# Five edits at the seams of a one-core transformer kernel: the last expert tile's order, the experts' numbers, the picks' weights, layer b's first batch, layer b's last root

## What is computed

```
x = x + attn_a(layernorm(x))        # 16 heads, causal
x = x + ffn(layernorm(x))           # 8 experts, each row goes to 2 of them
x = x + attn_b(layernorm(x))        # one head of 256, its own layernorm inside
x = x + ffn(layernorm(x))           # the same experts again

def ffn(x):
    t = x * rsqrt(mean(x * x) + EPS) * norm_scale
    top_v, top_i = top_k(t @ gate_w + gate_b, 2);  probs = softmax(top_v)
    for each expert e of a row: h = swiglu(t @ mlp1_w[e] + mlp1_b[e])
                                y += probs[e] * (h @ mlp2_w[e] + mlp2_b[e])
    return x + y
```

## Time and profile before

| | us |
|---|---|
| median of 3 runs (lowest, highest) | 1772.99 (1771.53, 1776.3) |
| the profiled execution: its own time | 1772.1 |
| its span | 1770.4 |
| PE busy in the span | 1627.7 (92%) |
| DVE busy | 1277.2 (72%) |
| ACT busy | 1046.8 (59%) |
| POOL busy | 801.5 (45%) |

### The profile page before, as it was taken

How to read it: one execution, slowest core, us unless ns; L and a number is a source line. 1 busy time by engine, 2 the same in 40 slices (tenths; PEclk the granted TensorE clock), 3 DMA queues, 4 the chain that set the end, 5 groups by cost and what they waited for, 6 DMA issues and landing times. The chain is left out here.

```text
span 1770.4 us, 35743 instructions
## 1 busy us (share of the span) xinstructions
PE 1627.7 (92%) x11140; PEld 1195.2 (68%) x11141; DVE 1277.2 (72%) x2668; ACT 1046.8 (59%) x1849; POOL 801.5 (45%) x773
## 2 busy tenths in 40 slices
PE   7889999999999784999999997799965999999997
PEld 3454444444443673999999997445444999999997
DVE  5678788888882686777777775368876777777775
ACT  3336677776777464666666663557653666666664
POOL 5431111112121132666666664225642666666674
PEclk9999999999999895999999999899975999999999
DMA  5755254453431662332322323301112223222232
GB/s 140 187 143 132 86 137 113 112 133 105 121 96 43 163 222 69 65 48 48 48 48 48 48 48 45 96 0 48 48 63 70 42 48 48 48 48 48 47 48 38
DMA packets 102668, 140.85 MB, mean 80 GB/s; under 512 B 18161, under 2 KB 86769, under 8 KB 99505
## 3 DMA queue, kind: packets, MB, share of 16 engines
q1 hardware_dynamic: 65638, 90.88, 19.3%
q0 software_dynamic: 31808, 37.32, 13.3%
q10 hardware_dynamic: 5130, 11.54, 1.9%
HBM read 74.21 MB, written 56.69 MB: 74 GB/s over the span
## 5 line engine op out<-in xcount | busy, mean ns | idle before, releaser
L555 ACT ACTIVATE a_Pt<-a_p_st 128x512 f32<-128x512 f32 (+2 forms) x624 | 301.6, 592 | 131.3 <-PE a_p_st L636 131.2
L582 DVE TENSOR_REDUCE mx<-a_p_sn 128x2 f32<-128x256 f32 (+1 forms) x600 | 332.9, 626 | 61.6 <-PE a_p_sn L619 52.2
L1322 ACT COPY R<-values_then_w 128x1024 f32 x284 | 283.0, 1044 | 41.7 <-issue 21.4
L1273 PE MATMUL e_p_g<-e_tT,R 128*128 128x128 f32 x2272 | 280.2, 277 | 3.4 <-ACT e_tT L1314 3.4
L1273 PE MATMUL e_p_l<-e_tT,R 128*128 128x128 f32 x2272 | 276.9, 275 | 0.0
L1285 PE MATMUL e_p_y<-w,e_hid 128*128 x1136 | 268.9, 380 | 2.3 <-DVE e_hid L1388 2.3
L1273 PEld LDWEIGHTS e_p_g<-e_tT,R 128*128 128x128 f32 x2272 | 268.0, 194 | 4.3 <-ACT e_tT L1314 4.2
L1273 PEld LDWEIGHTS e_p_l<-e_tT,R 128*128 128x128 f32 x2272 | 265.2, 192 | 0.0
L532 POOL TENSOR_SCALAR_AFFINE_SELECT a_Pt<-a_Pt 128x512 f32<-128x512 f32 x128 | 81.6, 637 | 361.9 <-ACT a_Pt L555 361.9
L1285 PEld LDWEIGHTS e_p_y<-w,e_hid 128*128 128x128 f32 x1136 | 205.0, 190 | 25.1 <-issue 3.1
L619 PE MATMUL a_p_sn<-Kst,Qst 96*128 96x128 bf16 (+1 forms) x720 | 219.0, 331 | 1.5 <-PEq L151 1.5
(11 more groups left out here) (211 smaller groups left out, 2375.0 us busy)
## 6 DMA issues: line engine op xcount, KB each, us to landing
qk_parts<-a_part SPq DMA_DIRECT2D x64, 192.0 KB, 3.1
a_Vst<-values_then_w SPq DMA_DIRECT2D x16, 512.0 KB, 18.4
o_rows<-a_OT ACTq DMA_DIRECT2D x32, 256.0 KB, 2.9
values_then_w<-in_mlp SPq DMA_DIRECT2D x16, 512.0 KB, 4.5
t_rows<-R SPq DMA_DIRECT2D x16, 512.0 KB, 3.0
Kst<-qk_parts SPq DMA_DIRECT2D x14, 384.0 KB
Qst<-qk_parts SPq DMA_DIRECT2D x14, 384.0 KB
X<-in_x SPq DMA_DIRECT2D x8, 512.0 KB, 5.4
```

The costliest lines, as they stand in the source:

```text
L555: act.activation(weights(kb, slice(h, h + n), a, b), p_st[:, i % RING, 0:n * (b - a)].rearrange("p (n w) -> p n w", n=n), ACT.Exp, scale=D ...
L582: dve.tensor_reduce(mx[:, hs[0]:hs[-1] + 1, place], p_sn[:, (s + k) % RING, 0:w * len(hs)].rearrange("p (h w) -> p h w", w=w), AX.X, ALU.m ...
L1273: mm = pe.matmul(bank[:, s, c * P:(c + 1) * P], copied[:, s, k, at:at + P], tT[:, s, k * P:(k + 1) * P], start=(k == 0), stop=(k == KD - 1))
L1322: act.copy(copied[:, s, :, cols], g["w1"][:, bass.ds(e, 1), :, cols].rearrange("p a k n -> p (a k) n")).then_inc(copied_done, 1)
```

## The change

- **The last expert tile's order.** In step 70 PE does `down(69)` between the two halves of `up`, and DVE makes `yb(69)` before it adds the bias to p_l. It was after both on either engine.
- **The experts' numbers.** The three instructions that make `expert` stand ahead of DVE's wait for `inv_done`, not at the list's end.
- **The picks' weights.** All weights are gathered by `load` in `experts`; those of tiles 0 and 1 were gathered in `rank`. They count on a semaphore `wt_in` of their own. PE's `rows` waits for the rows alone, and ACT's `result` has one more wait, for `wt_in`. SP waits for `w_out` in POOL's place.
- **Layer b's first batch in halves.** Norm 0's first unit of eight tiles becomes two of four, in statistics, moments, root, coefficients and normals; the later units' numbers go up by one. ACT begins the block with a square root of one element, which nobody reads.
- **Layer b's last root at once.** `deviations(1, B - 1)` stands ahead of `turned_rows(last // 2 + 1)`.

```diff
@@ rank, DVE
+            link(dve.tensor_tensor(tiles[:, :, :], g["ramp"][:, 0:MT].unsqueeze(2).to_broadcast([P, MT, E]),
+                                   cnt[:, 2, :].unsqueeze(1).to_broadcast([P, MT, E]), ALU.is_ge))
+            link(dve.tensor_reduce(fslot[:, :], tiles[:, :, :], AX.X, ALU.add))
+            link(dve.tensor_scalar(g["expert"][:, :], fslot[:, :], float(E - 1), None, ALU.min))
             dve.wait_ge(inv_done, Q // QQ)
...
             link(dve.tensor_tensor(g["result"][:, :], row[:, 1, :], g["spare"][:, :], ALU.add))
-            link(dve.tensor_tensor(tiles[:, :, :], g["ramp"][:, 0:MT].unsqueeze(2).to_broadcast([P, MT, E]),
-                                   cnt[:, 2, :].unsqueeze(1).to_broadcast([P, MT, E]), ALU.is_ge))
-            link(dve.tensor_reduce(fslot[:, :], tiles[:, :, :], AX.X, ALU.add))
-            link(dve.tensor_scalar(g["expert"][:, :], fslot[:, :], float(E - 1), None, ALU.min))
@@ rank, POOL
             pool.wait_ge(token_done, 1)
-            gather_rows(pool, g, t_dram, 0)
-            pool.wait_ge(pick_done, 1)
-            pool.wait_ge(w_out, 16)
-            gather_weight(pool, g, w_dram, 0)
-            gather_rows(pool, g, t_dram, 1)
-            gather_weight(pool, g, w_dram, 1)
+            for j in range(2):
+                gather_rows(pool, g, t_dram, j)
@@ gather_weight
-                            ).then_inc(g["xs_in"][j % 2], 16)
+                            ).then_inc(g["wt_in"][j % 2], 16)
@@ experts, POOL load
                 if j >= 2:
                     pool.wait_ge(tp_done, j - 1)
                     gather_rows(pool, g, t_dram, j)
-                    gather_weight(pool, g, w_dram, j)
+                gather_weight(pool, g, w_dram, j)
@@ experts, PE rows
-                pe.wait_ge(xs_in[s], 16 * (j - s) + 32)
+                pe.wait_ge(xs_in[s], 8 * (j - s) + 16)
@@ experts, PE step
+                if last:
+                    down(j - 1, 1 - s, e, False)
                 up(j, s, 1, p_l, copied_l, l_done, l_read, first)
-                if not begins:
+                if not begins and not last:
                     down(j - 1, 1 - s, e, isinstance(j, int) and j < 3)
@@ experts, ACT result
                 act.wait_ge(yb_done, j + 1)
+                act.wait_ge(g["wt_in"][s], 8 * (j - s) + 16)
@@ experts, DVE step
                 dve.tensor_scalar(glu[:, s, :], glu[:, s, :], LIMIT, None, ALU.min).then_inc(glu_done, 1)
+                if last:
+                    result(j - 1, 1 - s, expert_of(j - 1), False)
                 dve.wait_ge(l_done, j + 1)
@@ layer_b
-        if i < 2 or b < B - 1:
+        if i == 0:
+            return slice(4 * b, 4 * b + 4) if b < 2 else slice(QB * (b - 1), QB * b)
+        if i == 1 or b < B - 1:
             return slice(QB * b, QB * (b + 1))
...
+    def first_unit_of(j):
+        return j // 4 if j < QB else j // QB + 1
@@ layer_b, ACT
+            act.activation(table[:, :], g["eps"][:, :], ACT.Sqrt)
             for i, w in enumerate((Mw, Nw)):
...
-            deviations(0, 0)
-            for q in range(QB):
-                normal(q)
+            for half in range(2):
+                deviations(0, half)
+                for q in range(4):
+                    normal(4 * half + q)
...
             last, back = QB * (B - 2), QB * (B - 1)
+            deviations(1, B - 1)
             turned_rows(last // 2 + 1)
-            deviations(1, B - 1)
@@ layer_b, DVE
-            for q in range(QB):
-                first_statistics(q)
-            moments(0, 0)
-            coefficients(0, 0)
+            for half in range(2):
+                for q in range(4):
+                    first_statistics(4 * half + q)
+                moments(0, half)
+                coefficients(0, half)
```

More of the change, by code:

```diff
@@ L998, in rank @@
         mem.sem(s) for s in ("diff_d", "exp_d", "picks_d", "far_d", "cnt_d"))
-    b_in, ramp_done, slots_done, spread_done, row_done, tile_done, mark_done, inv_done, token_done, pick_done = (
-        mem.sem(s) for s in ("b_in", "ramp_d", "slots_d", "spread_d", "row_d", "tile_d", "mark_d", "inv_d", "token_d", "pick_d"))
+    b_in, ramp_done, slots_done, spread_done, row_done, tile_done, mark_done, inv_done, token_done = (
+        mem.sem(s) for s in ("b_in", "ramp_d", "slots_d", "spread_d", "row_d", "tile_d", "mark_d", "inv_d", "token_d"))
     w_done, wt_done, wT_done, w_out = (mem.sem(s) for s in ("w_d", "wt_d", "wT_d", "w_out"))
@@ L1009, in _ @@
             sp.wait_ge(b_in, 16)
+            sp.wait_ge(w_out, 16)
         @block.scalar
@@ L1121, in _ @@
             dve.tensor_scalar(g["pick"][:, :], coded, 16, 2 * T - 1, ALU.logical_shift_right, ALU.bitwise_and
-                              ).then_inc(pick_done, 1)
+                              )
             link(dve.tensor_scalar(used[:, :], p_inv[:, 0:MT], 0.5, None, ALU.is_ge))
@@ L1388, in step @@
                 dve.tensor_tensor(hid[:, s, :], lin[:, s, :], sig[:, s, :], ALU.mult).then_inc(hid_done, 1)
-                if not (first and s == 0):
+                if not (first and s == 0) and not last:
                     result(j - 1, 1 - s, even[0] if s == 1 else expert_of(j - 1), isinstance(j, int) and j < 3)
@@ L1415, in layer_b @@
     small = mem.sb("small", [P, 2, 5])
+    table = mem.sb("table", [P, 1])
     wn, wfT = square_weights(g)
@@ L1561, in normal @@
             def normal(j):
-                act.wait_ge(coef_done[0], j // QB + 1)
+                act.wait_ge(coef_done[0], first_unit_of(j) + 1)
                 if j >= 16:
@@ L1627, in _ @@
                         if b + 1 < B:
-                            deviations(0, b + 1)
+                            deviations(0, b + 2)
                     if q < 3 and b >= 2:
@@ L1679, in statistics @@
                 ins = dve.bn_stats(g["st6"][:, j, :], row)
-                if j == unit(i, unit_of(j) if i == 2 else j // QB).stop - 1:
+                if j == unit(i, (first_unit_of(j), j // QB, unit_of(j))[i]).stop - 1:
                     ins.then_inc(done, 1)
@@ L1770, in scaled @@
                                          in1=srep[:, :], op0=ALU.mult, op1=ALU.mult).then_inc(t_done, 1)
-            for q in range(QB):
-                first_statistics(q)
-            moments(0, 0)
-            coefficients(0, 0)
+            for half in range(2):
[3 more added lines that the diff above has]
+                coefficients(0, half)
             for q in range(QB, 2 * QB):
                 first_statistics(q)
-            moments(0, 1)
+            moments(0, 2)
             column_sums(0)
@@ L1795, in _ @@
                         if b + 1 < B:
-                            coefficients(0, b + 1)
+                            coefficients(0, b + 2)
                         if b >= 1:
@@ L1818, in _ @@
                     if q == 7 and b + 2 < B:
-                        moments(0, b + 2)
+                        moments(0, b + 3)
                     if j >= 1:
@@ L2097, in program @@
         g["xs_in"] = [keep.sem(f"xs_in1_{s}") for s in range(2)]
+        g["wt_in"] = [keep.sem(f"wt_in1_{s}") for s in range(2)]
         with ExitStack() as span:
@@ L2103, in program @@
         g["xs_in"] = [keep.sem(f"xs_in2_{s}") for s in range(2)]
+        g["wt_in"] = [keep.sem(f"wt_in2_{s}") for s in range(2)]
         with ExitStack() as span:
```

## The result

The changed kernel takes 1768.49 us (median of 21 runs, 1764.07 to 1796.04), the kernel before 1773.98 beside it (21 runs, 1769.95 to 1789.42). The ratio is 0.9972, with a 95% interval of 0.9958 to 0.9985: 0.28% or 5.0 us less, with 2.7 to 7.5 inside the interval. The forecast was -4.1 us and 1768.9. One run of the changed kernel, the one of 1796.04 us with a mean granted clock of 0.90 instead of 0.94 to 0.95, is left out of the ratio.

The account below looks back on a forecast made before the run. PE, fully busy at full clock in the experts' loops, bounds the kernel; only seams between phases can gain. -2.74 + 0 - 0.51 - 1.05 + 0.2 = -4.1 us, so 1768.9 for the median; range 1765.5 to 1772.5.

Parts of the forecast that it names:

- The experts' numbers: Both rankings' ends: DVE's list ends 1.37 us earlier, and ACT's first weight copy with it; -2.74 us for the two.
- The rival with another holder of the barrier: Rankings: DVE's end doesn't open the barrier, so moved numbers give nothing; sum -1.4, 1771.6 us; chance 0.20 shared with both tails cold.
- The picks' weights: Experts' loop and its start: the separate semaphore costs and gives nothing; 0 us, bounds -1.02 and +0.5.
- Layer b's first batch: Layer b's begin: table load hidden in ACT's wait for PE, second root and DVE's answer added; -0.51 us.
- the first half's lead: Layer b's begin: first four normals run 1.28 us earlier, as the table load is hidden.
- the second half's added 0.77: Layer b's begin: second root on ACT and DVE's answer, 0.30 + 0.47 us, ahead of the second four normals.
- the two bounds: Layer b's begin: -1.28 us if the added 0.77 were hidden, +0.77 if the table load stays where it was.
- Layer b's last root: Layer b's end: normals 2.0 us earlier, but PE's logits and transposes between two ACT copies cap the gain; -1.05 us.
- The last tile: Ends of both experts' loops: -0.7 us for a warm tail, +0.9 for a cold one; one of each taken, +0.2.
- cold tail: Last expert tile: PE's clock drops over the 2.84 us hole, the last down runs at the low clock; +0.9 us.
- ACT's added wait: Experts' loop: hidden in ACT's 0.96 us idle ahead of its sigmoid; rival: slower, 1776 at 1.01 us a wait, chance 0.05.

## Why the prediction was right

The sum was -4.1 and the measured ratio gives -5.0, with 2.7 to 7.5 inside its interval. Read just behind each edit, the seams give -5.0 too: 2 x -1.46 for the rankings, +0.1 for the two tails on average, -0.72 and -1.40 in layer b. But this match is partly luck. Read where the loop has its steady pace, the rankings are worth 2.2 and not 2.9, and of the 0.72 only 0.4 is seen at the layer's first exponential. What arrives is then 3.9 to 4.2, inside the interval as well. From DVE's last mark instruction of the first ranking to the span's end the kernel before takes 1079.3 and the changed one 1074.1, 1073.9 and 1078.0, on average 4.0 less. So the mechanisms were right, and the sum came near because the rankings were put too high and layer b's end too low. Step by step:

- **The experts' numbers, -2.74: right in place, too high in size** (-2.91 at the first `up`, -2.2 in the loop). The step took the first tiles' start for the end of the account; these tiles run in part at the low clock, and a lead won there was worth less later. The hole covered 1.43 of the three instructions, 0.34 spilled over, and DVE's end opens the barrier: SP, ACT and PE all came 1.45 earlier. The rival with another holder of the barrier is out.
- **The picks' weights, 0: right alone, wrong in company.** The step asked what the separate semaphore saves in the kernel before. It did not ask what the earlier barrier lets loose. SP's bias loads come forward with it and run into the weights' gather. Numbers alone cost 0.38 and 0.71; with the weights apart they gain 1.45 and 1.46. Made second, this edit is thus worth 1.8 and 2.2 us. The sum didn't suffer, since both edits are in it and the first one had been costed as if the wait were gone.
- **Layer b's first batch, -0.51: mechanism right, size small** (-0.72). The term that was off is the first half's lead, taken as 1.28, measured as 4.50 - 3.04 = 1.46; the second half's added 0.77 measured as (7.88 - 3.04) - (8.60 - 4.50) = 0.74. Of the two bounds one was seen: +0.71 without the early load (forecast +0.77). The load's full 1.28 alone was not to be had, because the moments of eight tiles come next. And 0.72 is what PE's turned group gains; further on 0.4 is seen, the rest is open.
- **Layer b's last root, -1.05: mechanism right, size small** (-1.40). The normals came 2.14 earlier (2.0 forecast) and PE's chain between the copies capped it at 1.14 (1.05). The other 0.27 lies behind the last copy. From it to the second normals it is 1.51 instead of 1.78; the root follows 0.49 instead of 0.62 behind it, and one of DVE's coefficient instructions takes 0.16 instead of 0.29. That one ran beside POOL's last gamma product before and runs behind it now. That POOL's work is what slowed it was not tested.
- **The last tile, +0.2 for one cold tail of two: right** (+0.03 a tail on average). At the full clock the store comes 0.4 to 0.6 earlier (0.7 forecast) where the store of tile 69 is on time: the handover from y takes 0.27, not 0.2, and the store of tile 69 lands about when y(70) is ready. Below it, it comes 1.0 to 1.1 later (13.57 and 13.73 against 12.59; 0.9 forecast), or 0.1 later where only a part of the `down` was slow (12.67). Three of eight tails ran below full clock, where the prediction took half; eight are too few to tell these shares apart. Unforeseen was a further case, full clock with a late store, which gives nothing (12.68) and stands beside a code load.
- **ACT's added wait, hidden: right.** 5.51 us a tile.

Three tails were slow behind 2.9 us without work, and none of 14 behind 1.16 and none of four behind 1.60. The Trainium skill's rule that activity releases PE's throttle (TensorE: Matmul & The Clock Gate, "What's actually happening") agrees with these counts. Five tails behind the same 2.9 us kept the full clock, and nothing here was done to find out what sets them apart.

The hole ahead of the transposes of tile 2 stays open. It was 1.02, 0.91, 0.53 or 0.48 in the second experts of four kernels, with the weights apart in one of them, and absent in the others; it is not the weights' wait alone.

## What to carry to other kernels

An edit that opens a barrier earlier lets every queue behind it start earlier, and their transfers may then collide with the one on the path: cost the pair, not each part. Where the end hangs on a chain of stores that wait for each other, what counts is when the last but one may start; an instruction moved on the engine that makes its data did more (0.71 a tail) than the swap on PE, which paid with a longer hole and its clock. To size an edit of a microsecond, measure from an instruction just ahead of the seam to one just behind it, not the span; then measure once more to an instruction where the pace is steady. A lead of 1.46 us at the first `up` was 1.1 by then, most likely because PE still ran at the low clock when it was won.

## What was not expected of the hardware

- In 14 profiles the first `token` starts between 693.1 and 708.6 us, in code that is the same in all; the granted clock from 590 us up to it is 0.81 in the earliest and 0.73 in the latest. From there to the span's end the kernel before takes 1077.3 and the changed one 1071.7, 1071.5 and 1075.6 (its `token` stands 0.34 later within the ranking). Most of the spread of these 14 spans, 1768.1 to 1785.4, thus lies ahead of the first `token`, in good part in `out_rows`, where PE falls to the low clock for longer or shorter.
- A gather of 128 single weights released PE 2.4 us after its issue with no bulk load beside it, and 3.8 us when eight loads of 128 KB were issued from 0.08 us ahead of it on.
- The spacing of two stores that wait for each other was 4.3 to 5.0 us, and twice 5.5, with the same instructions around them. In those two the packet of code of 16 KB was loaded in the midst of the first store's transfers.
